# Self-attention without transposes of weights, probabilities and values on TensorE: VectorE turns 32x32 blocks and DMAs inside SBUF place them

## The chip, the cores and the metric

One core of a Trainium2 chip. The metric is the device time of one execution in microseconds.

## The reference

One decoder layer over x of 4 x 512 x 512 in float32. Each of three parts is added to its input and normalised:

```python
k, q, v = W_K x, W_Q x, W_V x                 # 16 heads of 128, float32
scores = causal(q k^T); attn = softmax(scores / sqrt(128))
x = layernorm(x + W_O concat(attn v))
x = layernorm(x + gamma * xattn(x, ctx, ctx)) # 8 heads of 64
xq = activation_quant(rms_norm(x))
x = layernorm(x + (silu(xq sign(W_g)^T) * (xq sign(W_u)^T)) sign(W_d)^T)
```

## The kernel before

The program has four blocks with a barrier between them: constants, `attention` (a loop over 16 heads, four batch items in each, 64 items), `cross_attention` and `ffn`. All data of x stays in SBUF (`acc`). Each float32 operand of a matmul is held as two parts, `hi` (rounded to the matmul's format) and `lo` (the rest), and each product is three matmuls (`SPLIT`: hi hi, hi lo, lo hi).

The order of the work is written by hand, in one instruction stream for each engine; engines meet at semaphores. Every stream has a function `step(h, b)` that holds what it does for item `i = 4h + b`. What TensorE does in a step: the projections K and Q of the next item (12 matmuls of 512 columns each, L355), ten 128x128 transposes of the probabilities of this item (L430), the projection V, at b = 0 and 1 transposes of the signs of the feed-forward weights (L454), z = probabilities times values (L469), the scores of the next item (L368), four transposes of v (L361), and the output projection O (L487). At b = 2 and 3 it also transposes the four weight tiles of the next head (L346), 16 transposes a head. ScalarE copies each PSUM result into its `hi` part (L504) and makes the exponentials (L510); VectorE makes the `lo` parts (L581), turns scores into logits with their row maxima (L590), and adds the output into `acc` (L645). GpSimd does nearly nothing in this block. SP issues all loads; each weight tile is one DMA of 256 KB over 128 partitions.

The signs of the feed-forward weights are made during attention and kept in SBUF, as BF16 (`gT`, `uT`) and as 8-bit integers (`dT`), which ScalarE widens in the first batch of `ffn` (L1252).

The few lines of TensorE's step that set its order of waits:

```python
pe.wait_ge(exp_done, i * NT + NT)          # then the ten transposes
pe.wait_ge(pt_lo, i * len(PT_GROUPS) + (j + 1))   # then z, group by group
pe.wait_ge(z_lo, i + 1)                    # then O
```

## Time and profile before

| | us |
|---|---|
| median of 3 runs | 1622.2 |
| lowest and highest run | 1622.14 and 1622.71 |
| span of the profiled execution | 1621.2 |
| TensorE busy in it | 1574.0 |
| end of the attention stage in it | 1109.5 |

The profiled execution has a span from its first to its last instruction; what lies around the span in a run is 1.0 us by the median. Busy time of TensorE is the time in which some matmul is in its pipeline, so an engine that is always busy need not run at its peak. A wait of an engine that is not the bottleneck costs nothing.

### The profile page before, as it was taken

The page shows a single profiled execution, that of the slowest core. Times are in us where ns is not written, and L with a number is a line of the kernel's source. Part 1 is how long each engine was busy: PE and PEld are TensorE (multiplying, and loading weights), DVE is VectorE, ACT ScalarE, POOL GpSimd, SP SyncE. Part 2 cuts the span into 40 slices and gives each one's busy share as a digit, 9 for nine tenths or more (in the row PEclk, how much of TensorE's full clock was granted, in tenths as well). Part 3 has the DMA queues.
Part 4 walks back from the last instruction along what each step waited for, and adds up shares of the span by engine and source line. Part 5 has one row for each costly group of instructions (what it writes and reads, how often), then busy time and mean ns, then how long its engine had stood idle before and what let it go on. Part 6 is the DMA issues. An engine that isn't in the chain of part 4 may idle for free. (4 is left out here: it accounts for less than half of the span.)

```text
span 1621.2 us, 25726 instructions
## 1 busy us (share of the span) xinstructions
PE 1574.0 (97%) x8332; PEld 1270.9 (78%) x8352; DVE 1014.8 (63%) x2125; ACT 788.7 (49%) x1789; POOL 286.4 (18%) x301
## 2 busy tenths in 40 slices
PE   8999999999999999999999999997999998999997
PEld 7888888888888888888888888885887775565564
DVE  4555555555555555555555555567899996877854
ACT  5444444444444444444444444444888875433332
POOL 0000000000000000000000000004788872433432
PEclk9999999999999999999999999997999999999998
DMA  5000010100101001010010100011111100000000
GB/s 175 29 31 19 26 32 14 44 19 26 32 13 45 19 26 32 13 42 22 26 32 13 32 32 26 2 45 47 52 58 59 40 20 1 1 27 1 26 26 27
DMA packets 40393, 50.85 MB, mean 31 GB/s; under 512 B 3488, under 2 KB 19872, under 8 KB 40352
## 3 DMA queue, kind: packets, MB, share of 16 engines
q1 hardware_dynamic: 40352, 50.35, 9.7%
q8 instruction: 21, 0.34, 0.1%
q14 instruction: 20, 0.16, 0.0%
HBM read 46.14 MB, written 4.19 MB: 31 GB/s over the span
## 5 line engine op out<-in xcount | busy, mean ns | idle before, releaser
L162 POOL TENSOR_TENSOR norm_rstd<-norm_var_eps,minus_half 128x4 f32<-128x4 f32 x12 | 12.2, 1014 | 1116.2 <-DVE norm_var_eps L122 1116.2
L645 DVE SCALAR_TENSOR_TENSOR acc<-attn_bank,prob_recip,acc 128x512 f32<-128x512 f32 x256 | 179.7, 744 | 16.9 <-PE attn_bank L487 16.9
L510 ACT ACTIVATE probs<-probs,neg_max 128x128 f32<-128x128 f32 (+3 forms) x256 | 142.0, 557 | 61.7 <-DVE neg_max L590 61.7
L581 DVE TENSOR_TENSOR zT_lo<-attn_bank,zT_hi 128x512 fp32r<-128x512 f32 x64 | 44.3, 692 | 190.0 <-ACT zT_hi L504 190.0
L504 ACT CAST kT_hi<-attn_bank 128x512 fp32r<-128x512 f32 x64 | 37.5, 587 | 180.3 <-PE attn_bank L355 180.3
L581 DVE TENSOR_TENSOR qT_lo<-attn_bank,qT_hi 128x512 fp32r<-128x512 f32 x64 | 44.2, 691 | 126.0 <-ACT qT_hi L504 125.9
L581 DVE TENSOR_TENSOR kT_lo<-attn_bank,kT_hi 128x512 fp32r<-128x512 f32 x64 | 44.3, 692 | 122.9 <-ACT kT_hi L504 122.9
L1195 PE MATMUL y_bank<-wdT_f32r,prod_hi 128*128 128x512 f32 x256 | 110.8, 433 | 3.0 <-POOL prod_lo L1136 2.5
L1136 POOL TENSOR_TENSOR prod_lo<-prod,prod_hi 128x512 fp32r<-128x512 f32 x64 | 85.6, 1337 | 142.1 <-ACT prod_hi L1244 142.1
L590 DVE CUSTOM_DVE_ANT_0 probs<-attn_bank,mask 128x128 f32<-128x128 f32 (+3 forms) x256 | 109.8, 485 | 0.1
L487 PE MATMUL attn_bank<-woT_hi,zT_hi 128*128 128x512 f32 x256 | 106.2, 415 | 1.6 <-DVE zT_lo L581 1.4
L892 ACT ACTIVATE xprobs<-x_bank,xneg_max 128x512 f32<-128x512 f32 x128 | 88.4, 690 | 38.1 <-DVE xneg_max L956 37.7
L785 POOL TENSOR_SCALAR xprobs<-xprobs,xprob_recip 128x512 f32<-128x512 f32 x128 | 99.5, 793 | 36.5 <-DVE xprob_recip L965 36.5
L504 ACT CAST qT_hi<-attn_bank 128x512 fp32r<-128x512 f32 x64 | 37.7, 589 | 134.7 <-PE attn_bank L355 134.7
L581 DVE TENSOR_TENSOR pT_lo<-attn_bank,pT_hi 128x384 fp32r<-128x384 f32 (+1 forms) x192 | 101.7, 584 | 0.0
L1195 PE MATMUL y_bank<-wdT_f32r,prod_lo 128*128 128x512 f32 x256 | 101.2, 395 | 0.0
L504 ACT COPY vT<-attn_bank 128x512 f32<-128x512 f32 x64 | 37.6, 587 | 129.8 <-PE attn_bank L355 129.8
L487 PE MATMUL attn_bank<-woT_hi,zT_lo 128*128 128x512 f32 x256 | 100.7, 393 | 0.0
L487 PE MATMUL attn_bank<-woT_lo,zT_hi 128*128 128x512 f32 x256 | 99.9, 390 | 0.0
L961 DVE TENSOR_TENSOR xpT_lo<-x_bank,xpT_hi 128x512 fp32r<-128x512 f32 x128 | 87.5, 685 | 7.7 <-ACT xpT_hi L897 5.1
L956 DVE TENSOR_REDUCE xneg_max<-x_bank 128x1 f32<-128x512 f32 x128 | 87.3, 682 | 7.6 <-PE x_bank L826 7.0
L1244 ACT CAST prod_hi<-prod 128x512 fp32r<-128x512 f32 x64 | 39.6, 619 | 99.7 <-DVE prod L1281 98.9
(149 smaller groups left out, 4176.1 us busy)
## 6 DMA issues: line engine op xcount, KB each, us to landing
rows_twice<-in_ctx_dram SPq DMA_DIRECT2D x64, 128.0 KB, 2.6
rows<-in_L_attn_W_K_dram SPq DMA_DIRECT2D x16, 256.0 KB, 2.6
rows<-in_L_attn_W_Q_dram SPq DMA_DIRECT2D x16, 256.0 KB, 2.9
rows<-in_L_attn_W_V_dram SPq DMA_DIRECT2D x16, 256.0 KB, 3.4
rows<-in_L_attn_W_O_dram SPq DMA_DIRECT2D x16, 256.0 KB, 2.7
rows_twice<-in_L_ffn_W_g_dram SPq DMA_DIRECT2D x16, 256.0 KB, 2.7
rows_twice<-in_L_ffn_W_u_dram SPq DMA_DIRECT2D x16, 256.0 KB, 2.8
rows_twice<-in_L_ffn_W_d_dram SPq DMA_DIRECT2D x16, 256.0 KB, 2.7
```

The costliest lines, as they stand in the source:

```text
L487: last_mm = nc.tensor.matmul(O_BANK[t][:], zT[zp][:, t * P:(t + 1) * P], wT["wo"][wp][:], start=(n == 0), stop=(n == 2))
L504: nc.scalar.copy(out, bank[:, 0:cols]).then_inc(done, 1)
L510: nc.scalar.activation(probs[:, cols], probs[:, cols], ACT.Exp, bias=low[:, par, t:t + 1], scale=-1.0, accum_out=total[:, par, t:t + 1]).t ...
L581: nc.vector.tensor_tensor(parts[1][:, at:at + cols], bank[:, 0:cols], parts[0][:, at:at + cols].bitcast(F32), ALU.subtract).then_inc(done, 1)
L590: nc.vector.tensor_tensor_reduce(out=probs[:, s_at[t]:s_at[t] + n], in0=score_bank[bank][:, col:col + n], in1=k.mask[:, S - n:S], scale=-S ...
L645: nc.vector.scalar_tensor_tensor(out=acc[:, b * NT + t, :], in0=O_BANK[t][:], scalar=recip[:, par, t:t + 1], in1=acc[:, b * NT + t, :], op ...
L785: nc.gpsimd.tensor_scalar(probs[q][:, t, :], probs[q][:, t, :], recip[:, q, t:t + 1], 1.0, ALU.mult, ALU.mult).then_inc(probs_ready, 1)
L892: nc.scalar.activation(probs[q][:, t, :], score_bank[t % 2][:], ACT.Exp, bias=negmax[:, q, t:t + 1], accum_out=total[:, q, t:t + 1]).then_ ...
L956: nc.vector.tensor_reduce(negmax[:, q, t:t + 1], score_bank[t % 2][:], AX.X, ALU.max, negate=True).then_inc(max_ready, 1)
L961: nc.vector.tensor_tensor(pT[1][:, jt, :], pt_bank[jt][:], pT[0][:, jt, :].bitcast(F32), ALU.subtract).then_inc(pt_lo, 1)
L1136: nc.gpsimd.tensor_tensor(pT[i][1][:], prod[i][:], pT[i][0][:].bitcast(F32), ALU.subtract).then_inc(p_lo, 1)
L1195: last = nc.tensor.matmul(y_bank[n][:], pT[i][p][:, n * P:(n + 1) * P], wdT[:, t * D:(t + 1) * D], start=(t == 0 and p == 0), stop=(t == N ...
```

## The change

TensorE now transposes only x (at the start) and the quantised activations in `ffn`. Every other transpose is made in two steps. VectorE turns each 32x32 block in place in its 128x128 block (`turn_probs`, `turn_v`, `turn_weight`, `turn_ffn`). Then the 4 x 4 grid of blocks has to be placed: for weights this is done by the load from DRAM, which is now four DMAs over 32 partitions each; for the probabilities and v of an item (ten and four 128x128 blocks, tile `turned`) by 16 DMAs from SBUF to SBUF into `pv..._lo`, each over 32 partitions with 14 runs of 32 floats (128 bytes) in each partition. ScalarE then copies what landed into `pv_hi`, and GpSimd subtracts in place to get `pv_lo`, in two pieces of eight and six blocks. `turned` and both `pv` tiles exist twice. Items are made two ahead (`AHEAD`), one more than before.

The lo parts of weights move to GpSimd too. The signs of the feed-forward weights go to DRAM as they are made and are read back: gate and up at the start of cross-attention, down (as float32) at the start of `ffn`. x and the activations are split into chunks by every fourth column instead of by blocks of 128 columns (`chunk_of`).

```diff
+def chunk_of(x, c):
+    return x.rearrange("p (n c) -> p c n", c=NC)[:, c, :]
...
+        turned = [sb(f"turned{i}", [P, NBLK * P]) for i in range(2)]
+        pv = [[sb(f"pv{i}_{p}", [P, NBLK * P], F32R) for p in ("hi", "lo")] for i in range(2)]
+        zT = [sb(f"zT_{p}", [P, S], F32R) for p in ("hi", "lo")]
+        w_turned = [sb(f"w_turned{i}", [P, D]) for i in range(2)]
+        f_turned = sb("f_turned", [P, D])
...
-        pT = [sb(f"pT_{p}", [P, NPAIR], F32R) for p in ("hi", "lo")]
...
+            def load_projection(eng, name, w, h):
+                w_h = w[bass.ds(h, 1), :, :].rearrange("o (a s) (e j) -> e s (o a) j", s=R, e=E)
+                for e in range(E):
+                    eng.dma_start(raw[name][e * R:(e + 1) * R, :].rearrange("s (a j) -> s a j", a=E),
+                                  w_h[e]).then_inc(w_loaded[name], 16)
...
+            def load_output(eng, h):
+                for e in range(E):
+                    eng.dma_start(raw["wo"][e * R:(e + 1) * R, :].rearrange("s (g r) -> s g r", r=R),
+                                  wo[:, bass.ds(h * DH + e * R, R)].rearrange("(g s) r -> s g r", s=R)).then_inc(w_loaded["wo"], 16)
...
             @block.sync
             def _(sp):
...
+                def exchange(i, par):
...
+                    sp.wait_ge(p_turn, i + 1)
+                    for a in range(E):
+                        for c in range(E):
+                            sp.dma_start(pv[par][1][c * R:(c + 1) * R, :].bitcast(F32).rearrange("r (n a s) -> r n a s", a=E, s=R)[:, :, a, :],
+                                         turned[par][a * R:(a + 1) * R, :].rearrange("r (n c s) -> r n c s", c=E, s=R)[:, :, c, :]).then_inc(landed, 16)
...
+                def keep_signs(h, m):
+                    sp.wait_ge(signed, h * 3 + (m + 2))
+                    if m < 2:
+                        sp.dma_start(signs.gu[m][:, :, bass.ds(h * P, P)], sign_gu[m][:]).then_inc(signs_kept, 16)
+                    else:
+                        sp.dma_start(signs.d[:, bass.ds(h * D, D)], sign_d[:]).then_inc(signs_kept, 16)
...
+                def step(h, b, last):
+                    if not (last and b == B - 1):
+                        exchange(h * B + b + 1, (b + 1) % 2)
+                    if b > 0:
+                        keep_signs(h, b - 1)
+                    if b == 0 and not last:
+                        load_projection(sp, "wk", wk, h + 1)
+                        load_projection(sp, "wq", wq, h + 1)
+                    if b == 1:
+                        wait_apart(sp, k, f_turn, h * 3 + 1)
+                        load_down(sp, h)
+                        if not last:
+                            load_projection(sp, "wv", wv, h + 1)
+                            load_output(sp, h + 1)
+                    if b == B - 1 and not last:
+                        wait_apart(sp, k, f_turn, h * 3 + 3)
+                        load_gate_up(sp, "wg", h + 1)
+                        load_gate_up(sp, "wu", h + 1)
...
             @block.gpsimd
             def _(pool):
...
+                def pieces_lo(i, par):
+                    hi, low = pv[par]
+                    for g, (first, end) in enumerate(PIECES):
+                        cols = slice(first * P, end * P)
+                        pool.wait_ge(pv_hi, i * len(PIECES) + (g + 1))
+                        nc.gpsimd.tensor_tensor(low[:, cols], low[:, cols].bitcast(F32), hi[:, cols].bitcast(F32),
+                                                ALU.subtract).then_inc(pv_lo, 1)
...
             @block.tensor
             def _(pe):
-                def transpose_weights(name, bank):
-                    for c in range(NC):
-                        last = nc.tensor.transpose(bank[:, c * P:(c + 1) * P], raw[name][:, c * P:(c + 1) * P], k.ident[:])
-                    last.then_inc(proj_full, 1)
...
-                def transpose_v(bank):
-                    for j in range(NT):
-                        last = nc.tensor.transpose(bank[:, j * P:(j + 1) * P], vT[:, j * P:(j + 1) * P], k.ident[:])
-                    last.then_inc(proj_full, 1)
+                    last.then_inc(full, 1)
...
                 def step(h, b, last):
-                    more = not (last and b == B - 1)
-                    nb = (b + 1) % B
...
+                    more = not (last and b + AHEAD >= B)
+                    nb = (b + AHEAD) % B
...
-                    pe.wait_ge(exp_done, i * NT + NT)
-                    for g, js in enumerate(PT_GROUPS):
-                        for j in js:
-                            for t in range(j, NT):
-                                at = pt_at[j] - pt_at[js[0]] + (t - j) * P
-                                lt = nc.tensor.transpose(score_bank[g][:, at:at + P],
-                                                         probs[:, s_at[t] + j * P:s_at[t] + (j + 1) * P], k.ident[:])
-                        lt.then_inc(pt_full, 1)
...
-                    if b < 2:
-                        name = ("ffn_gu", "ffn_d")[b]
-                        pe.wait_ge(signed, h * 2 + (b + 1))
...
-                        bank = bank_of(b, name, last)[:].bitcast(BF16)
-                        for m in range((2, 1)[b]):
-                            for c in range(NC):
-                                at = (m * NC + c) * P
-                                lt = nc.tensor.transpose(bank[:, at:at + P], sign_ffn[:, m, c * P:(c + 1) * P], k.ident16[:])
-                        lt.then_inc(proj_full, 1)
...
+                    pe.wait_ge(z_lo, i + 1)
...
-                        if j < len(PT_GROUPS):
-                            pe.wait_ge(pt_lo, i * len(PT_GROUPS) + (j + 1))
+                        if j < len(PIECES):
+                            pe.wait_ge(pv_lo, i * len(PIECES) + (j + 1))
...
-                            last_mm = nc.tensor.matmul(z_bank[:, j * P:S], v[vp][:, j * P:(j + 1) * P],
-                                                       pT[pp][:, pt_at[j]:pt_at[j] + (NT - j) * P],
+                            last_mm = nc.tensor.matmul(z_bank[:, j * P:S], pv[b % 2][vp][:, V_AT[j] * P:(V_AT[j] + 1) * P],
+                                                       pv[b % 2][pp][:, 4 * j * P:(3 * j + NT) * P],
...
                     if more:
-                        pe.wait_ge(proj_lo, lo_count(h, b, "q", last))
-                        scores()
...
+                    pe.wait_ge(z_lo, i + 2)
...
+                    if not (last and b == B - 1):
+                        pe.wait_ge(logits_ready, i * NT + 2 * NT)
...
+                    if more:
+                        pe.wait_ge(v_turn, i + AHEAD)
+                        if new:
+                            pe.wait_ge(w_lo["wv"], h + 2)
+                        project("wv", nb, v_bank, v_full)
...
+                        pe.wait_ge(o_added, i * NT + NT)
+                        scores()
...
             @block.scalar
             def _(act):
...
+                def pieces_hi(i, par):
+                    act.wait_ge(landed, i * (16 * E * E) + 16 * E * E)
+                    for first, end in PIECES:
+                        cols = slice(first * P, end * P)
+                        nc.scalar.copy(pv[par][0][:, cols], pv[par][1][:, cols].bitcast(F32)).then_inc(pv_hi, 1)
...
                 def step(h, b, last):
...
+                    more = not (last and b + AHEAD >= B)
+                    if not (last and b == B - 1):
+                        exps(i + 1, (b + 1) % 2)
                     if more:
-                        group(h, b, "k", last)
...
+                    act.wait_ge(z_full, i + 1)
+                    hi(zT[0][:], z_bank, z_hi)
                     if more:
...
+                        act.wait_ge(q_full, i + AHEAD + 1)
+                        hi(qT[0][:], q_bank, q_hi)
...
+                    if not (last and b == B - 1):
+                        pieces_hi(i + 1, (b + 1) % 2)
...
             @block.vector
             def _(dve):
...
+                def turn_weight(name, n):
...
+                    if not (isinstance(n, int) and n + before == 1):
+                        dve.wait_ge(w_lo[other], n - 1 + before)
+                    dve.wait_ge(w_loaded[name], n * (16 * E))
+                    nc.vector.transpose(*turn_views(w_turned[TMP[name]][:], raw[name][:], name != "wo")).then_inc(w_turn[name], 1)
...
+                def turn_probs(i, par):
+                    for t in range(NT):
+                        dve.wait_ge(exp_done, i * NT + (t + 1))
+                        last = nc.vector.transpose(blocks(turned[par][:], t, 3, t + 1),
+                                                   blocks(probs[:, s_at[t]:s_at[t] + (t + 1) * P], 0, 1, t + 1))
+                    last.then_inc(p_turn, 1)
...
+                def turn_v(i, par, first):
...
+                    dve.wait_ge(v_full, i + 1)
+                    if not first:
+                        dve.wait_ge(landed, i * (16 * E * E) - 16 * E * E)
+                    nc.vector.transpose(blocks(turned[par][:], V_AT[0], V_AT[1] - V_AT[0], 2), blocks(v_bank[:], 0, 1, 2))
+                    nc.vector.transpose(blocks(turned[par][:], V_AT[2], V_AT[3] - V_AT[2], 2), blocks(v_bank[:], 2, 1, 2)).then_inc(v_turn, 1)
...
                 def step(h, b, last):
...
+                    if not (last and b == B - 1):
+                        turn_probs(i + 1, (b + 1) % 2)
+                    if b == 1 and not last:
+                        turn_weight("wk", h + 2)
+                        turn_weight("wq", h + 2)
...
+                        lo(kT, k_bank, k_hi, i + AHEAD + 1, k_lo)
...
+                    lo(zT, z_bank, z_hi, i + 1, z_lo)
+                    if more:
+                        lo(qT, q_bank, q_hi, i + AHEAD + 1, q_lo)
...
-                    for g, js in enumerate(PT_GROUPS):
-                        dve.wait_ge(pt_hi, i * len(PT_GROUPS) + (g + 1))
-                        lo(pT, score_bank[g], pt_at[js[0]], sum(P * (NT - j) for j in js), pt_lo)
...
+                    if b == 1 and not last:
+                        turn_weight("wv", h + 2)
+                    if b == 2 and not last:
+                        turn_weight("wo", h + 2)
+                    if b < 3:
+                        turn_ffn(("wg", "wu", "wd")[b], h, b)
+                    if more:
+                        turn_v(i + AHEAD, par, False)
+                        rows_of_scores(i + AHEAD, par)
...
+                signs.load(sp)
...
+                for t in range(NHT):
+                    sp.dma_start(wdT[:, t * D:(t + 1) * D].bitcast(F32), signs.d[:, t * D:(t + 1) * D]).then_inc(wd_loaded[t], 16)
...
-                            last = nc.tensor.transpose(bank[:, at:at + P], xq[:, t, c * P:(c + 1) * P], k.ident16[:])
+                            last = nc.tensor.transpose(bank[:, at:at + P], chunk_of(xq[:, t, :], c), k.ident16[:])
...
-                        if first:
-                            nc.scalar.copy(wdT[:, t * D:(t + 1) * D], dT[:, t * D:(t + 1) * D]).then_inc(wd_ready, 1)
```

How the order of instructions changed is shown at four places. TensorE before, in the step of the first item: from projection Q of the next item to the transposes of signs (`probs` are the probabilities, `ident` the unit matrix of a transpose).

```order
L355 MATMUL attn_bank<-xT_hi,wqT_lo 128x512 x4
L425 ISA
L430 MATMUL attn_bank<-ident,probs 128x128 x10
L273 REGISTER_ALU
L355 MATMUL attn_bank<-xT_hi,wvT_hi 128x512 x4
L355 MATMUL attn_bank<-xT_lo,wvT_hi 128x512 x4
L355 MATMUL attn_bank<-xT_hi,wvT_lo 128x512 x4
L448 ISA
L273 REGISTER_ALU
L454 MATMUL attn_bank<-ident,sign_ffn 128x128 x8
```

TensorE now, in the same step, between the last matmuls of z and the first of O (`pv` holds the turned probabilities and values).

```order
L466 MATMUL attn_bank<-pv_lo,pv_hi 128x128
L466 MATMUL attn_bank<-pv_hi,pv_lo 128x128
L406 MATMUL attn_bank<-xT_hi,wqT_hi 128x512 x4
L406 MATMUL attn_bank<-xT_lo,wqT_hi 128x512 x4
L406 MATMUL attn_bank<-xT_hi,wqT_lo 128x512 x4
L477 REGISTER_ALU
L479 ISA
L484 MATMUL attn_bank<-woT_hi,zT_hi 128x512
```

No transposes stand there any more; projection Q has moved between z and O, and V and the scores follow behind O.

ScalarE now, in the step b = 1, from the copy of z to the exponentials of the next item (`probs` written with `prob_sum`).

```order
L506 CAST zT_hi<-attn_bank 128x512
L506 CAST qT_hi<-attn_bank 128x512
L512 CAST wqT_hi<-w_turned 128x512
L522 ISA
L525 CAST pv_hi<-pv_lo 128x1024
L525 CAST pv_hi<-pv_lo 128x768
L517 ISA
L518 ACTIVATE probs,prob_sum<-probs,neg_max 128x128
```

Before, the copies of transposed probabilities stood between the projections' copies, each waiting for TensorE. Now one wait (the ISA row at L522) for the 16 transfers stands ahead of the two copies, and the exponentials of the next item follow them.

SP now, in the step b = 1: the 16 transfers, the store of signs, then loads for `wd`, W_V and W_O of the next head.

```order
L298 DMA pv_lo<-turned 32x14x32 x16
L309 ISA
L311 ISA
L311 DMA sign_g_kept<-sign_g 512x1x128
L70 ISA
L288 REGISTER_ALU
L288 DMA rows_twice<-in_L_ffn_W_d_dram 32x16x32
...
L271 DMA rows<-in_L_attn_W_V_dram 32x4x128 x4
L276 ISA
L276 DMA rows<-in_L_attn_W_O_dram 32x16x32
```

Before, SP issued 7 loads in a whole head and one for each tile.

VectorE now, in the step b = 1, from the lo part of z to the turn of v (`w_turned<-rows` is the turn of W_V, and waits for its load).

```order
L695 SCALAR_TENSOR_TENSOR acc<-attn_bank,prob_recip,acc 128x512 x4
L609 STREAM_TRANSPOSE w_turned<-rows 128x512
L612 REGISTER_ALU
L614 STREAM_TRANSPOSE f_turned<-rows_twice 128x512
L640 ISA
L641 STREAM_TRANSPOSE turned<-attn_bank 128x2x128
L642 STREAM_TRANSPOSE turned<-attn_bank 128x2x128
L70 ISA
L621 ISA probs,neg_max<-attn_bank,mask 128x128
```

Before, the scores of the next item were reduced ahead of the adds into `acc`. Now the turns of W_V and of signs stand between the adds and the turn of v, behind which the scores of the item after next are reduced.

## Rows read from the trace of the kernel before

**Rows 1.** The page, part 1: busy us, share of the span, instructions.

```profile
PE 1574.0 (97%) x8332; PEld 1270.9 (78%) x8352; DVE 1014.8 (63%) x2125; ACT 788.7 (49%) x1789; POOL 286.4 (18%) x301
```

**Rows 2.** Windows: us, busy by engine, TensorE clock, DMA share, GB/s.

```profile
0.00:29.68 29.68, 22.91 (x132) 20.04 (x133) 14.15 (x23) 13.60 (x24) 1.97 (x12) 1.00 0.66 230
97.20:164.70 67.50, 67.50 (x371) 57.75 (x370) 36.45 (x84) 30.45 (x73) 0.00 (x0) 1.00 0.09 27
1109.50:1356.50 247.00, 230.23 (x1217) 182.03 (x1216) 225.87 (x408) 193.05 (x447) 186.72 (x213) 0.94 0.15 45
```

**Rows 3.** Waits of the attention stage, 30 to 1109 us: total, times, longest.

```profile
DVE zT_lo L581 <- ACT zT_hi L504: 190.0, 64, 4.0
...
PE attn_bank L469 <- DVE pT_lo L581: 1.1, 1, 1.1
```

**Rows 4.** Timeline of TensorE, one item: start, us, then what ran.

```profile
506.04 1.17 PE L355 MATMUL attn_bank<-xT_hi,wkT_hi 128*128 128x512 f32 x4
...
508.87 1.07 PE L355 MATMUL attn_bank<-xT_hi,wqT_hi 128*128 128x512 f32 x4
...
511.60 1.25 PE L430 MATMUL attn_bank<-ident,probs 128*128 128x128 f32 x10
512.61 1.17 PE L355 MATMUL attn_bank<-xT_hi,wvT_hi 128*128 128x512 f32 x4
...
515.43 0.62 PE L454 MATMUL attn_bank<-ident,sign_ffn 128*128 128x128 bf16 x8
515.86 0.48 PE L469 MATMUL attn_bank<-pT_hi,v_hi 128*128 128x512 f32 x1
...
517.80 0.28 PE L368 MATMUL attn_bank<-kT_hi,qT_hi 128*128 128x128 f32 x1
...
519.77 0.60 PE L361 MATMUL attn_bank<-ident,vT 128*128 128x128 f32 x4
520.12 0.48 PE L487 MATMUL attn_bank<-woT_hi,zT_hi 128*128 128x512 f32 x1
...
522.98 1.07 PE L355 MATMUL attn_bank<-xT_hi,wkT_hi 128*128 128x512 f32 x4
```

**Rows 5.** Groups by line: busy, mean ns of one, idle before.

```profile
L510 ACT ACTIVATE probs<-probs,neg_max 128x128 f32<-128x128 f32 (+3 forms) x256 | 142.0, 557 | 61.7 <-DVE neg_max L590 61.7
...
L538 ACT ACTIVATE sign_ffn<-rows_twice 128x1024 bf16<-128x1024 f32 x8 | 8.5, 1063 | 0.0
...
L581 DVE TENSOR_TENSOR zT_lo<-attn_bank,zT_hi 128x512 fp32r<-128x512 f32 x32 | 22.2, 692 | 97.6 <-ACT zT_hi L504 97.6
...
L1136 POOL TENSOR_TENSOR prod_lo<-prod,prod_hi 128x512 fp32r<-128x512 f32 x64 | 85.6, 1337 | 142.1 <-ACT prod_hi L1244 142.1
```

**Rows 6.** SP's DMA issues: timeline, then min/median/max ns by line, then landing.

```profile
3.98 1.85 SPq L286 DMA_DIRECT2D acc<-in_x_dram  x4
...
1067.31 2.47 SPq L98 DMA_DIRECT2D rows_twice<-in_ctx_dram  x4
...
L94 SPq DMA_DIRECT2D rows<-in_ctx_dram x16: 327/341/505, 1052.7 to 1244.1; - x16
...
L98 SPq DMA_DIRECT2D rows_twice<-in_ctx_dram x64: 465/547/600, 1067.3 to 1317.2; - x64
...
rows_twice<-in_ctx_dram SPq DMA_DIRECT2D x64, 128.0 KB, 2.6
```

**Rows 7.** Windows: the load of one W_O tile (512 packets), and the first loads.

```profile
507.40:509.20 1.80, 1.80 (x10) 1.48 (x9) 0.34 (x1) 0.59 (x2) 0.00 (x0) 1.00 0.58 152
8.00:24.00 16.00, 15.43 (x85) 13.58 (x86) 10.60 (x17) 8.52 (x16) 0.00 (x0) 1.00 1.01 361
```

**Rows 8.** Timeline at the start of cross-attention, SP and GpSimd.

```profile
1113.56 2.79 SPq L98 DMA_DIRECT2D rows_twice<-in_ctx_dram  x4
...
1121.55 0.62 POOL L770 TENSOR_SCALAR cp_hi<-rows_twice 128x512 fp32r<-128x512 f32 x1 [2.83 <-PE x_bank L826]
```

**Rows 9.** Window at the start of cross-attention.

```profile
1110.00:1138.00 28.00, 19.61 (x53) 12.58 (x54) 18.92 (x38) 13.65 (x31) 18.20 (x19) 0.52 0.26 76
```

More of the change, by code:

```diff
@@ L530, in step @@
+                pieces_hi(0, 0)
                 def step(h, b, last):
[L531 removed]
                     i = h * B + b
[L533 to L538 removed]
@@ new lines, in step @@
+                    if b == 2 and not last:
+                        weight_hi("wv", h + 2)
+                    if b > 0:
+                        act.wait_ge(f_turn, h * 3 + b)
+                        act.wait_ge(signs_kept, h * 48 + (16 * b - 15))
+                        if b < 3:
+                            out, x = sign_gu[b - 1][:].rearrange("p c (a s) -> p c a s", a=E), by_chunk(f_turned[:])
+                        else:
+                            out, x = sign_d[:], f_turned[:]
+                        nc.scalar.activation(out, x, ACT.Sign).then_inc(signed, 1)
@@ L1203, in _ @@
                 spread_steps(0)
+                pe.wait_ge(signs.loaded, 32)
                 def batch(b, first, last):
```

546 lines of the change are left out of this document (239 added, 307 removed).

## Prediction

> **What bounds the kernel now.** I read the busy line first, then the stages, then the waits, then one item on TensorE. TensorE is busy for 97% of the span [rows 1]. By stage [rows 2] a head of self-attention takes 67.5 us and TensorE is busy for all of it at granted clock 1.00; cross-attention has 230 of 247 us. The waits of the attention stage say the same from the other side: VectorE idles 190 us in 64 waits for zT_hi alone, while TensorE's one wait for pT_lo is 1.1 us long [rows 3]. So an item of attention costs what its matmuls cost. The profiled span is 1621.2 us, 1.0 us below the median of 1622.2 of the three runs; the sum is made against 1621.2 and 1.0 is added at the end. Faster or slower by 0.2% (3.2 us) is about what such runs can tell from no change.
>
> **TensorE's part.** From the starts in [rows 4], an item is K 2.8, Q 2.7, ten turns of probs 1.0, V 2.8, eight turns of signs 0.4, z 1.9, scores 2.0, four turns of v 0.35, O 2.9. The first matmul behind turns takes some 0.1 longer than its neighbours, so without turns a projection is 2.73, z 1.86, O 2.76, and the item of the changed kernel is 3 x 2.73 + 1.86 + 1.97 + 2.76 = 14.8 us, a head 59.2. Turns, signs and weights thus give back 67.5 - 59.2 = 8.3 us a head, 133 us in 16 heads, if nothing else is late.
>
> **The new path, and the ring it closes.** Between scores and z now stand VectorE, SP's queue, ScalarE and GpSimd. ScalarE works in order: it copies the landed pieces of one item (pieces_hi) and only then makes the exponentials of the next. So one ring runs once per item: landing, two copies, four exponentials, last turn, 16 transfers, landing. Its terms:
> - two copies of 1024 and 768 columns: the sign of 1024 columns took 1.06 us [rows 5], so 1.9 for both.
> - four exponentials of a mean 0.56 [rows 5], which follow one another closely: 2.4 with their gaps.
> - the last turn_probs, 512 columns. No row shows VectorE turning blocks. From below stands the subtraction of 128x512, 0.69 [rows 5], from above twice that, if four-byte blocks run at half rate. I take 0.65 for what delays the ring, since both are one pass over 512 columns; the other end adds 0.6 a ring.
> - a transfer of 57 KB from its issue to landing: 2.6 as the 128 KB loads [rows 6]; that needs its own packets not to be the limit (rival C).
> - 15 issue pitches p on SP. Four 128-partition loads took 1.85 us, so (1.85 - 0.43)/3 = 0.47 apart; four 64-partition loads took 2.47, so (2.47 - 0.59)/3 = 0.63 apart [rows 6]. The median issue is 0.34 against 0.55 us, though the 64-partition load moves half the bytes. The new transfers have 32 partitions, so the 64-partition row is nearest and I take 0.63; 0.47 is the lower end. No row has 32 partitions.
> With handoffs of 0.1 the ring is 7.6 + 15p: 17.0 at 0.63, 14.7 at 0.47. At 0.63 it exceeds TensorE's 14.8; at 0.47 they tie.
>
> The Trainium skill, "VectorE: DVE Perf Modes", section "The three transpose paths", gives 311 ns for a 128x128 two-byte block; by that figure, an estimate, the four blocks of the last turn take up to 1.24, the ring grows by 0.6, and the sum becomes 37 us larger. No run here shows a turn yet.
>
> **What stands behind a new wait.** In step b=1 SP issues 16 transfers, one store of signs, four loads for wd, then four of wv. VectorE, in the same step, waits for that wv load before it turns wv and wu, turns v and reduces the next scores (turn_weight stands ahead of them). At p = 0.63 SP starts 5.0 us into the step, the 25th issue is 24 x 0.63 = 15.1 later and lands 2.6 later, at 22.7; VectorE has finished the adds at 13.9. It waits 9 us, and the turns, the v turn, the reductions, last exponential and last turn of the item behind it (5.7) end at 28.4 where the ring wanted 22.1: 6.3 us late once a head. At 0.47 the same working gives 2.5 + 11.3 + 2.6 = 16.4, then 22.1 against 17.3; slack eats a little, 4.5 remain. Heads: 4 x 17.05 + 6.3 = **74.5**, or 4 x 14.8 + 4.5 = 63.7.
>
> **Ends of the stage.** The loop began at 29.7. Two items are now made ahead, which adds 3 x 2.73 + 1.97 = 10.2; twenty turns of weights and v go, -2.1; the first weights pass SP's and ScalarE's issues, VectorE, ScalarE and GpSimd (its 128x512 subtraction is 1.34 [rows 5]) before the first projection: some 9. Loop start 47. The first z waits 7 more. Two items in the last head have no K, Q, V and scores, -20.3, but their waits for z are uncovered, +8. End: 47 + 7 + 16 x 74.5 - 20.3 + 8 = 1234, against 1109.5: **+124**.
>
> **Behind attention.** The signs of gate and up, 4 MB, are read back ahead of the context rows. At the 361 GB/s of the first loads [rows 7] that keeps the DMA engines for 11.6 us. The GpSimd split that needs rows issued at 1113.6 ran at 1121.6 [rows 8], so 8 of it are covered and 4 to 5 show: +5 (0 to 11). The down signs, 16 loads at the start of the feed-forward, land before use; the 16 casts that ScalarE loses there were beside TensorE: 0. Turning x by every fourth column is a strided weight load that no row shows; 128 such turns, 0 to +6, taken as 0. Stores of signs: hidden, SP time counted above.
>
> **Sum.** 1621.2 + 124 + 5 + 1 = **1751**. With p within 0.60 to 0.66 this case spans 1710 to 1790.
>
> **Rivals.**
> - **B, the issues are quick.** p is 0.47, as for full-width loads. For it: the burst of full-width loads has it, and it is what is left if the width of a transfer does not matter. Against it: every 64-partition row is at 0.47 to 0.60 for the issue alone. Then 45 + 7 + 16 x 63.7 - 20.3 + 9 = 1060, 50 us sooner: 1621.2 - 50 + 5 + 1 = **1577**. The sign turns at p = 0.51, since 0.16 us of p are worth 174. The whole 133 less the ends would be 1503, with p below 0.4 and no wait for wv.
> - **C, small packets are the bound.** A transfer is 448 packets of 128 bytes, 28 for each of the 16 DMA engines. 512 packets of 512 bytes took at most 1.80 x 0.58 x 16 / 512 = 33 ns each [rows 7]. If a 128-byte packet costs as much, a transfer occupies the engines 0.92 us, the ring is 5.0 + 16 x 0.92 + 2.2 = 22 us, a head 91, and the time 1751 + 16 x 16.5 = **2015**. Scaled by bytes alone it would be 0.23 and hidden by p. It decides from 22 ns up. Against it: cost should fall with size at least in part. The Trainium skill, "DMA: Bandwidth & Descriptors", section "Specifications", says that packets under 512 bytes go through a read-modify-write; the same page, in "Why small descriptors are slow (HBM only)", exempts transfers within SBUF. By the first this case is right, by the second it is out; no trace shown here decides.
> - **D, the clock falls.** TensorE is idle a fifth of the time in my case, with waits of 3 to 4 us. Behind the waits at the start of cross-attention the granted clock was 0.52 for 28 us [rows 2, 9], the lower level of 1.2 GHz. One such stretch a head costs 6 to 11 us a head beyond slack: 1850 to 1930. Against it: waits of 1 us at the end of attention changed nothing.
> - **E, it balances** within 0.2%: p within 0.003 of 0.51.
>
> **Chances.** My case 0.45, B 0.31, C 0.13, D 0.08, E 0.03. So faster 0.31, same 0.03, slower 0.66. The range has to reach into B for its 0.31 and up into D; 1560 to 1900 leaves out C (0.13), a quarter of D and about 0.04 of B.
>
> **What would show it.** Right: SP rows of the 16 transfers 0.6 apart, TensorE waiting 2 us before each z for pv_lo, a head near 74 us, VectorE waiting some 9 us for wv once a head, and more DMA packets (7168 an item) at a share under half. B: pitch 0.47, heads near 64. C: DMA share near 1 in the exchanges and landings that grow over the 16. D: a clock below 1.0 in attention. If heads are at 59 the ring is wrong altogether.

## The result, and the profile after

| | before | after |
|---|---|---|
| median, us | 1622.17 (4 runs, 1620.06 to 1622.71) | 1758.14 (4 runs, 1757.77 to 1761.85) |
| ratio to before | | 1.0852, 95% interval 1.0837 to 1.0867 |
| profiled span, us | 1621.2 | 1760.0 |
| start of the loop, us | 29.7 | 56.4 |
| one head in the steady part, us | 67.5 | 74.1 |
| end of self-attention, us | 1109.5 | 1244.8 |
| the rest, us | 511.7 | 515.2 |

The kernel became 8.5% slower: 136 us, against the 129 forecast, and inside the likeliest case's own range of 1710 to 1790. The line numbers below are the changed kernel's, and its copies of landed pieces are line 525.

The page, part 1 (busy us, share of the span, instructions), answers to [rows 1]:

```profile
PE 1526.5 (87%) x7008; PEld 1178.6 (67%) x7008; DVE 1111.8 (63%) x2303; ACT 711.4 (40%) x1549; POOL 637.1 (36%) x493
```

TensorE lost 1324 matmuls and is busy 47 us less, but over a span 139 us longer: no engine is full now. The windows of the start and of one head answer to [rows 2] (us, busy by engine, granted clock, DMA share, GB/s):

```profile
0.00:56.42 56.42, 34.49 (x160) 28.67 (x161) 21.65 (x47) 15.24 (x31) 5.79 (x15) 0.97 0.42 108
493.85:567.97 74.12, 64.34 (x294) 51.66 (x293) 44.07 (x98) 26.10 (x59) 21.85 (x12) 0.98 0.47 81
```

In a head TensorE is idle for 9.8 of 74.1 us; before it was idle for none. The waits (total, times, longest) say for what:

```profile
ACT pv_hi L525 <- DMA pv_lo<-turned: 456.4, 64, 11.0
...
DVE w_turned L609 <- DMA rows<-in_L_attn_W_V_dram: 121.4, 15, 9.0
PE attn_bank L466 <- POOL pv_lo L372: 103.3, 114, 7.7
```

The first two rows shown are the two things that the prediction built on: ScalarE waiting for each of the 64 landings, and VectorE waiting once a head for wv. The long idle time of [rows 3], VectorE's 190 us for z, has shrunk to 92.

The ring, the closed chain of waits that every item goes round once, can be read off three timelines (start us, us, what ran, and in brackets the idle time before it). ScalarE's copies of the landed pieces, one head:

```profile
493.85 1.78 ACT L525 CAST pv_hi<-pv_lo 128x1024 fp32r<-128x1024 f32 x2 [10.38 <-DMA pv_lo<-turned]
510.68 1.78 ACT L525 CAST pv_hi<-pv_lo 128x1024 fp32r<-128x1024 f32 x2 [6.57 <-DMA pv_lo<-turned]
527.48 1.78 ACT L525 CAST pv_hi<-pv_lo 128x1024 fp32r<-128x1024 f32 x2 [6.57 <-DMA pv_lo<-turned]
544.27 1.79 ACT L525 CAST pv_hi<-pv_lo 128x1024 fp32r<-128x1024 f32 x2 [6.01 <-DMA pv_lo<-turned]
567.97 1.79 ACT L525 CAST pv_hi<-pv_lo 128x1024 fp32r<-128x1024 f32 x2 [10.39 <-DMA pv_lo<-turned]
```

Three periods of 16.8 and one of 23.7 make the head of 74.1. Between the second and the third row, ScalarE:

```profile
512.37 0.40 ACT L518 ACTIVATE probs<-probs,neg_max 128x128 f32<-128x128 f32 x1
...
514.57 0.56 ACT L506 CAST kT_hi<-attn_bank 128x512 fp32r<-128x512 f32 x1
```

And SP's queue, whose row of 16 is the exchange of one item:

```profile
515.43 10.62 SPq L298 DMA_DIRECT2D pv_lo<-turned  x16
...
532.23 10.61 SPq L298 DMA_DIRECT2D pv_lo<-turned  x16
543.11 0.63 SPq L311 DMA_DIRECT2D sign_g_kept<-sign_g  x1
544.12 1.95 SPq L288 DMA_DIRECT2D rows_twice<-in_L_ffn_W_d_dram  x4
546.16 1.86 SPq L271 DMA_DIRECT2D rows<-in_L_attn_W_V_dram  x4
...
555.88 10.66 SPq L298 DMA_DIRECT2D pv_lo<-turned  x16
```

So the ring from 510.68 to 527.48 is: copies 1.7, exponentials 2.2, last turn 0.9 (514.57 to 515.43), from the first issue to the start of the last 10.0 (the row's 10.62 less one issue of 0.62, the median), landing 2.05. Sum 16.8. The exception is the item after 544.27. VectorE's own row for it, and the turns of probabilities behind it:

```profile
549.83 1.11 DVE L609 STREAM_TRANSPOSE w_turned<-rows 128x512 f32<-128x512 f32 x1 [8.51 <-DMA rows<-in_L_attn_W_V_dram]
...
554.14 1.72 DVE L632 STREAM_TRANSPOSE turned<-probs 128x128 f32<-128x128 f32 x4
```

The wv load ends with the 25th issue, at 548.0, and has landed at 549.8; everything behind it on VectorE, the reductions that ScalarE's exponentials need among it, is late, and the exchange starts at 555.88.

### The profile page after: what moved, and what is told of

Its sections match the earlier page's. It is cut to its first block and busy times, and to the rows that moved or that the text cites. A ratio compares the mean times of both kernels' runs of the same rounds, so it can differ in the third digit from the quotient of the medians.

```text
span 1760.0 us, 24483 instructions
## 1 busy us (share of the span) xinstructions
PE 1526.5 (87%) x7008; PEld 1178.6 (67%) x7008; DVE 1111.8 (63%) x2303; ACT 711.4 (40%) x1549; POOL 637.1 (36%) x493
## 5 line engine op out<-in xcount | busy, mean ns | idle before, releaser
L372 POOL TENSOR_TENSOR pv_lo<-pv_lo,pv_hi 128x1024 fp32r<-128x1024 f32 (+1 forms) x128 | 267.7, 2113 | 685.2 <-ACT pv_hi L525 685.2
L525 ACT CAST pv_hi<-pv_lo 128x1024 fp32r<-128x1024 f32 (+1 forms) x128 | 114.2, 940 | 456.4 <-DMA pv_lo<-turned 456.4
L466 PE MATMUL attn_bank<-pv_hi 128*128 128x512 f32 (+3 forms) x256 | 96.0, 375 | 103.5 <-POOL pv_lo L372 103.3
L632 DVE STREAM_TRANSPOSE turned<-probs 128x128 f32<-128x128 f32 (+3 forms) x256 | 124.6, 504 | 87.4 <-ACT probs L518 81.4
L484 PE MATMUL attn_bank<-woT_hi,zT_hi 128*128 128x512 f32 x256 | 115.2, 450 | 66.5 <-DVE zT_lo L595 66.5
L466 PEld LDWEIGHTS attn_bank<-pv_hi 128*128 128x128 f32 x256 | 51.7, 202 | 154.6 <-POOL pv_lo L372 142.9
L609 DVE STREAM_TRANSPOSE w_turned<-rows 128x512 f32<-128x512 f32 x64 | 61.8, 983 | 130.8 <-DMA rows<-in_L_attn_W_V_dram 121.4
L484 PE MATMUL attn_bank<-woT_lo,zT_hi 128*128 128x512 f32 x256 | 112.9, 441 | 0.0
L484 PEld LDWEIGHTS attn_bank<-woT_hi,zT_hi 128*128 128x128 f32 x256 | 55.4, 216 | 85.1 <-issue 66.7
L484 PE MATMUL attn_bank<-woT_hi,zT_lo 128*128 128x512 f32 x256 | 112.0, 438 | 0.0
```

The costliest lines, as they stand in the source:

```text
L372: nc.gpsimd.tensor_tensor(low[:, cols], low[:, cols].bitcast(F32), hi[:, cols].bitcast(F32), ALU.subtract).then_inc(pv_lo, 1)
L466: last_mm = nc.tensor.matmul(z_bank[:, j * P:S], pv[b % 2][vp][:, V_AT[j] * P:(V_AT[j] + 1) * P], pv[b % 2][pp][:, 4 * j * P:(3 * j + NT) ...
L484: last_mm = nc.tensor.matmul(s_bank[t][:], zT[zp][:, t * P:(t + 1) * P], wT["wo"][wp][:], start=(n == 0), stop=(n == 2))
L525: nc.scalar.copy(pv[par][0][:, cols], pv[par][1][:, cols].bitcast(F32)).then_inc(pv_hi, 1)
L632: last = nc.vector.transpose(blocks(turned[par][:], t, 3, t + 1), blocks(probs[:, s_at[t]:s_at[t] + (t + 1) * P], 0, 1, t + 1))
```

## The experiments

The kernel before was timed beside each. Its medians beside the timed runs were 1620.35 to 1621.61 (1618.42 in one run beside E6).

### E1: the wv load one step earlier

```diff
                     if b == 0 and not last:
...
                         load_projection(sp, "wq", wq, h + 1)
+                        load_projection(sp, "wv", wv, h + 1)
                     if b == 1:
...
-                            load_projection(sp, "wv", wv, h + 1)
                             load_output(sp, h + 1)
```

> Only the four loads of wv are moved, from behind the loads of wd in step b=1 to behind those of wk and wq in step b=0. Theory 1 (a ring of landing, copies, exponentials, turn and 16 issues, 16.8 us, and once a head the wait of VectorE for wv stretches it to 23.7): the wait (9 us, 15 times) is gone, all four periods are 16.8, the head 67.2 to 68, and the time 1758 - 16 x 6.5 = 1654, within 1640 to 1665. Theory 2 (SP's queue is full over the head, 64 transfers and 28 other issues, and the wait for wv only shows it): the four issues now push the exchange of step b=1 back by what they save later, and the time stays within 1750 to 1765.

Measured: 1654.47 us, ratio to before 1.0207 (1.0190 to 1.0224). In the steady part all periods are now 16.8; two of ScalarE's copies:

```profile
502.91 1.79 ACT L525 CAST pv_hi<-pv_lo 128x1024 fp32r<-128x1024 f32 x2 [6.07 <-DMA pv_lo<-turned]
519.75 1.78 ACT L525 CAST pv_hi<-pv_lo 128x1024 fp32r<-128x1024 f32 x2 [6.62 <-DMA pv_lo<-turned]
```

The single place of one load was worth 103.7 us. Only 15 of the 16 heads load weights for a next one (the wait for wv is there 15 times), so that is 6.9 for each of them, what the long period had over the others. The same number of issues stands on SP's queue, so theory 2 falls: it is not the load of the queue but who waits behind which issue.

### E6: what an issue costs

Bursts alone, no layer. The kinds differ in the pair of views given to each transfer.

> The layer is left out; only bursts of 16 transfers of 56 KB (one kind 28 KB) follow one another, each kind twice, each burst awaited before the next: (1) 32 partitions x 14 pieces of 128 bytes between quadrants, as the changed kernel has them, (2) the same with 7 pieces, (3) 32 partitions x one run of 1792 bytes, (4) 128 partitions x one run of 448 bytes, (5) 64 partitions x 14 pieces, twice the bytes, (6) 32 x 14 pieces read from DRAM in one run a partition; then (1) on ScalarE's queue, and at the end half of it on each queue at once. Theory A (the number of partitions sets the issue, as the prediction reasoned): (1), (2), (3), (6) have the same pitch, 0.6 to 0.7, and (4) 0.47. Theory B (the number of packets that an issue makes sets it): (2) and (3) are at 0.35 to 0.5, (1) and (6) at 0.6 to 0.7, (5) above 1.0. Packets: 12 ns each by the busy share of 0.52 in an exchange of 10.5 us, so (5) is bound by packets at 16 x 896 / 16 x 12 ns = 10.9 us, no longer than its issues. Last burst: two queues together take 5.5 to 6 us if packets bound it, 5.3 if issues do, 10.6 if the queues share one path.

Each burst's second run, in the timeline of SP (start us, us, what ran; 16 issues each, the last row 8), in order: 14 pieces, 7 pieces, one run of 1792 bytes, 128 partitions x 448 bytes, 64 partitions x 14 pieces, from DRAM, half of the 14 pieces on SP:

```profile
18.65 10.59 SPq L1468 DMA_DIRECT2D landing<-turned  x16
42.29 10.35 SPq L1468 DMA_DIRECT2D landing<-turned  x16
65.62 10.00 SPq L1468 DMA_DIRECT2D landing<-turned  x16
88.46 10.12 SPq L1468 DMA_DIRECT2D landing<-turned  x16
112.93 11.30 SPq L1468 DMA_DIRECT2D landing<-turned  x16
135.92 8.13 SPq L1468 DMA_DIRECT2D landing<-in_x_dram  x16
170.68 5.62 SPq L1468 DMA_DIRECT2D landing<-turned  x8
```

ScalarE's queue, with all of the 14 pieces alone, and with its half beside SP's last row:

```profile
158.43 10.76 ACTq L1468 DMA_DIRECT2D landing<-turned  x16
170.62 5.39 ACTq L1468 DMA_DIRECT2D landing<-turned  x8
```

Neither theory holds. Half the packets, a fourteenth of them, or four times the partitions change the pitch by 6% at most (0.67, 0.65, 0.63, 0.64), and twice the partitions and bytes cost 0.71. Of the kinds tried only the one that reads from DRAM is quicker: 0.52. Two queues issue at once at 0.72 and 0.68. DRAM as the source is not enough for a quick issue, though: the 64-partition context loads of [rows 6] read from it too and are 0.63 apart. Windows over the same bursts (the share is the last number but one), for the 14 pieces, the 7 pieces, the one run, 128 partitions, 64 partitions, and both queues:

```profile
18.65:31.00 12.35, 0.00 (x0) 0.00 (x0) 1.00 0.45 74
42.29:54.00 11.71, 0.00 (x0) 0.00 (x0) 1.00 0.24 39
65.62:77.00 11.38, 0.00 (x0) 0.00 (x0) 1.00 0.33 81
88.46:100.00 11.54, 0.00 (x0) 0.00 (x0) 1.00 0.29 80
112.93:125.90 12.97, 0.00 (x0) 0.00 (x0) 1.00 0.84 142
170.68:177.70 7.02, 0.00 (x0) 0.00 (x0) 1.00 0.81 131
```

A DMA engine gets 448 packets in the first: 12.35 x 0.45 / 448 = 12.4 ns for one of 128 bytes; 11.71 x 0.24 / 224 = 12.5 and 12.97 x 0.84 / 896 = 12.2 for the 7 pieces and the 64 partitions. That is the price of rival C, which needed 22. The same bytes in runs of 1792 bytes keep the engines busy for 11.38 x 0.33 = 3.8 us, in runs of 448 bytes for 11.54 x 0.29 = 3.3, in pieces of 128 bytes for 12.35 x 0.45 = 5.6: small packets cost 1.5 to 1.7 times as much here, but the 10.0 us of issues hide it. One exchange occupies the engines for 5.6 us, so two queues at 8 issues each are almost at that bound as well: share 0.81.

### E2 and E3: half of the transfers on ScalarE's queue

`exchange_part(eng, i, par, parts)` is the old `exchange` over some source quadrants; SP calls it for 0 and 1.

```diff
                         exps(i + 1, (b + 1) % 2)
+                        exchange_part(act, i + 1, (b + 1) % 2, range(2, E))
                     if more:
                         act.wait_ge(k_full, i + AHEAD + 1)
```

> Half of the 16 transfers of an item (source quadrants 2 and 3) are issued by ScalarE, right behind its four exponentials, the other half by SP as before. Theory 1 (the pitch of the issues on one queue bounds the ring): 8 x 0.665 = 5.3 us leave the ring, 11.5 is below TensorE's 14.8, and a head takes 60 to 63 us: time 1530 to 1580. Theory 2 (the packets bound it: 16 DMA engines are busy for 0.52 of 10.5 us in an exchange, 5.5 us for 448 packets each): two queues finish no sooner than the engines can, but 5.5 us is still half of 10.6, so the ring is near 12 and the time is the same within 10 us; had the busy share hidden waits inside the engines (a packet bound below 1.0), the landing would stay 12 us behind the first issue and the time at 1740 to 1760. Theory 3: ScalarE's own issues of 5.3 us delay its copies of k and q, and the head stays above 68: 1660 or more.

> The edits of the wv load and of the two queues together. Theory 1: TensorE sets the pace with 14.8 us an item, a head 59.5 to 61, and the time is 1515 to 1545, below the kernel before (1622). Where the granted clock stays near 1.0, the lower end. Rival (clock): TensorE still meets the lower clock behind its waits and the head stays above 64: 1590 or more.

Measured: E2 1872.75 us (ratio 1.156, 1.1538 to 1.1582), E3 (with E1's edit) 1875.74 (1.1562, 1.1541 to 1.1582). Both are slower than the changed kernel, and 0.2% apart: E1's edit gives nothing here. ScalarE in E2:

```profile
495.42 0.40 ACT L520 ACTIVATE probs<-probs,neg_max 128x128 f32<-128x128 f32 x1 [7.02 <-DVE neg_max L625]
...
498.65 5.69 ACTq L295 DMA_DIRECT2D pv_lo<-turned  x8
504.45 0.59 ACT L508 CAST kT_hi<-attn_bank 128x512 fp32r<-128x512 f32 x1 [6.59 <-issue]
...
505.99 0.57 ACT L508 CAST zT_hi<-attn_bank 128x512 fp32r<-128x512 f32 x1
...
515.90 0.40 ACT L520 ACTIVATE probs<-probs,neg_max 128x128 f32<-128x128 f32 x1 [6.66 <-DVE neg_max L625]
```

ScalarE no longer waits for a landing but for the next scores. The issues hold up the copy of z, which TensorE had ready at 500.6; its output projection waits for it, at 507.42:

```profile
507.42 0.78 PE L486 MATMUL attn_bank<-woT_hi,zT_hi 128*128 128x512 f32 x1 [3.87 <-DVE zT_lo L599]
508.00 0.63 PE L486 MATMUL attn_bank<-woT_lo,zT_hi 128*128 128x512 f32 x1
508.43 0.63 PE L486 MATMUL attn_bank<-woT_hi,zT_lo 128*128 128x512 f32 x1
```

A new ring: exponentials, turn, 8 issues, four copies, O, V, scores, reduction, exponentials: 20.5 us from 495.42 to 515.90. Theory 3 was right in kind and too small: it counted the copy of z with those of k and q, and not what TensorE still has to run behind it. The output projection also starts with matmuls 0.43 us apart, where they are 0.23 apart at clock 1.00: behind the wait of 3.9 the granted clock was 0.52 (507.42 to 510.94), the lower level.

### E5: the exponentials ahead of the copies

```diff
                         exps(i + 1, (b + 1) % 2)
+                    pieces_hi(h * 2 + (b // 2 + 1), b % 2)
...
-                    if not (last and b == B - 1):
-                        pieces_hi(i + 1, (b + 1) % 2)
```

> ScalarE makes the exponentials of item i+1 ahead of the copies of the landed pieces of item i (its wait for the landing moves behind them; one landing count for each parity). Theory 1 as forecast (the ring closes through ScalarE's order alone): with it broken an item costs TensorE's 14.8, or SP's 13 to 14 of issues, the head 60 to 66 with the wv wait, time 1535 to 1630. Theory 2 (behind it lies a second ring, from the scores through reduction 0.7, exponentials 2.2, turn 0.8, issues 10.6, landing 2.2, copy 0.95 and split 2.1 to z, two steps later and 2.7 into the step): about 17.9 + 0.5 - 2.7 = 15.7 an item, a head 63 plus 4 to 7 for wv, 67 to 70, time 1650 to 1695. Theory 3 (SP's queue bounds): no change, 1750 to 1765.

Measured: 1897.59 us, 1.1716 (1.1688 to 1.1744), a miss of all three theories. ScalarE:

```profile
499.18 0.40 ACT L518 ACTIVATE probs<-probs,neg_max 128x128 f32<-128x128 f32 x1 [5.98 <-DVE neg_max L619]
...
501.53 1.77 ACT L525 CAST pv_hi<-pv_lo 128x1024 fp32r<-128x1024 f32 x2
...
522.91 0.40 ACT L518 ACTIVATE probs<-probs,neg_max 128x128 f32<-128x128 f32 x1 [7.69 <-DVE neg_max L619]
```

And TensorE's first matmul of z:

```profile
505.08 0.50 PE L466 MATMUL attn_bank<-pv_hi 128*128 128x512 f32 x1 [2.41 <-POOL pv_lo L372]
```

The last issue for these pieces had ended at 493.7, 7.9 us before their copy began at 501.53. But z could now start only behind the exponentials and the copies of its pieces, 5.9 us after 499.18, and the scores of the next item stand behind z, Q, O and V in TensorE's order: 14 to 18 us more. Four items in a row took 19.5, 23.7, 19.9 and 20.0. In the one of 23.7, shown here, VectorE also waits 1.7 us for wv, and TensorE ran at granted clock 0.50 from 506.86 to 512.60, so that its projection Q took 4.8 us instead of 2.8. The order of the changed kernel, copies first, was the better one. Breaking one ring closed another.

### E7 and E9: the same issues where ScalarE idles

In the changed kernel ScalarE idles 2.2 us between the copies of z and q and 6.6 behind the copy of q. Both kernels have E1's edit, and SP issues the transfers that ScalarE does not. E7:

```diff
+                        exchange_part(act, i + 1, (b + 1) % 2, range(3, E))
                         pieces_hi(i + 1, (b + 1) % 2)
```

> The wv load in step b=0 as in e1_wv_early; the four transfers of the last source quadrant are issued by ScalarE at the end of its step, behind its copy of q and ahead of its wait for the landing, where it idled 6.6 us in e1_wv_early; SP issues the other 12. Theory 1 (issues on one queue bound the ring, and e2_two_queues lost because 5.7 us of issues stood ahead of the copies of k, z and q): SP's last issue comes 7.3 us behind its first instead of 10.0, ScalarE's last 7.6 behind it, the landing 2.2 later: the ring falls from 16.8 to 14.7, TensorE's 14.8 takes over, a head is 59.5 to 62 and the time 1654 - 16 x 6.3 = 1553, within 1535 to 1580, below the kernel before (1622). Theory 2 (two queues at once slow each other, as landings of 3.5 us in e2_two_queues against 2.2 may say): the landing comes 1.3 later, ring 16.0, time 1654 - 16 x 3 = 1605, 1590 to 1630. Theory 3 (z's wait for the split of the pieces is on TensorE's own path whatever the ring): above 1640.

Measured: **1534.17 us**, ratio 0.9467 (0.9452 to 0.9483). E9 counts `parts` in single transfers:

```diff
                     hi(zT[0][:], z_bank, z_hi)
+                    if not (last and b == B - 1):
+                        exchange_part(act, i + 1, (b + 1) % 2, range(10, 13))
...
+                        exchange_part(act, i + 1, (b + 1) % 2, range(13, E * E))
                         pieces_hi(i + 1, (b + 1) % 2)
```

> As e7_act_4, but SP issues 10 transfers, ScalarE three between its copies of z and q (2.2 us idle there) and three behind the copy of q. Theory 1: the last issue is 6.9 us behind SP's first, ring 14.0, below TensorE's 14.8, so TensorE alone sets the pace: head 59.5 to 61, time 1530 to 1560, and at or up to 15 us below e7_act_4. Rival: the three issues of 0.7 ahead of the copy of q delay q, and with it the scores of the item two ahead: slower than e7_act_4 by up to 64 x 0.6 = 40 us.

Measured: **1524.43 us**, ratio 0.9416 (0.9392 to 0.9440): 5.8% below the kernel before, and the fastest here. The window of one head of E9:

```profile
493.18:552.53 59.35, 59.16 (x289) 50.18 (x289) 42.03 (x96) 27.26 (x59) 22.11 (x12) 1.00 0.61 101
```

TensorE is busy for 59.16 of 59.35 us, at clock 1.00: the 59.2 that the prediction worked out for an item without turns. E7 missed its forecast of 1553 on the good side, because it counted 60.9 us a head, and a head took 59.8, TensorE busy for all but 0.05 of it. Two queues at once do slow the landing (a median of 2.7 and 2.8 us in E9, 2.2 in the changed kernel), but the slack covers that: what lost in E2 was not the second queue as such. The Trainium skill, "Perfetto Trace Analysis", section "DMA Optimizations", advises to balance transfers over the engines that can issue them when making descriptors is the limit. E9 agrees with it, with 1524 us; E2, with 1873, shows what it leaves out.

### E10: E9 with the wv load back in its place

> As e9_act_3_3, but the wv load is back where the changed kernel has it (step b=1, behind the loads of wd). Theory 1: in that step SP starts 4.9 us in, its 19th issue (10 transfers, a store, 4 for wd, 4 for wv) is 11.5 later and lands 2.0 after that, at 18.4; VectorE is free at 13.9, waits 4.5, and the exchange behind it starts 4 us later than TensorE alone would have it: 1524 + 16 x 4 = 1588, within 1565 to 1600. Rival: without the ring this wait lies in slack: under 1535.

Measured: 1585.41 us, 0.9778 (0.9761 to 0.9794), 61 us above E9, 4.1 for each of the 15 heads that load a next wv. The copies start at 494.23, 509.33, 523.75, 538.14 and 557.30: one period of 19.2 among three of 14.4 to 15.1. The wait for wv costs even where no ring bounds, only less: 4.1 us a head here, 6.9 in E1's comparison.

### E11: eight of the transfers late on ScalarE

E3 with `exchange_part(act, ...)` moved to the place that it has in E7.

> As e3_both (wv early, 8 of the 16 transfers issued by ScalarE), but ScalarE issues them at the end of its step, behind the copy of q, as in e7_act_4. Theory 1 (e3_both lost by the place of the issues, not by their number or by two queues at once): the copies of k, z and q are free again; ScalarE's last issue comes 5.5 + 7 x 0.7 = 10.4 us behind SP's first, where SP alone had 10.0, so the ring is about 17.2 and the time 1654 + 64 x 0.4 = 1680, within 1650 to 1710. Theory 2 (eight transfers on each of two queues slow each other): near e3_both, above 1800.

Measured: 1754.19 us, 1.0821 (1.0784 to 1.0859). The place alone gave back 121 us of E3's 1875.74, but the forecast of 1680 was 74 too low. Two neighbouring items (windows: us, busy by engine, granted clock, DMA share, GB/s):

```profile
504.78:525.33 20.55, 17.70 (x72) 14.43 (x71) 10.26 (x23) 6.13 (x14) 5.38 (x3) 0.83 0.47 83
486.60:504.78 18.18, 17.07 (x82) 13.84 (x81) 10.60 (x28) 6.16 (x15) 4.20 (x2) 1.00 0.53 94
```

One ran at clock 1.00 in 18.2 us, the other at 0.83 in 20.5. ScalarE's eight issues stand behind the copy of q and end the exchange, so TensorE's z and Q are inside the ring. (With four, in E7, SP's last issue was the later one: 480.56 against 480.10 in one item.) In the slower item z follows a wait of 2.0 us, and the copy of q comes 4.6 us behind that of z instead of 2.8. This is rival D at work, in a ring that passes through TensorE.

The clock is the smaller part of the miss, though. Of 62 periods in the stage, 36 ran at clock 1.00 and still took 18.1 us on average, 0.9 above the forecast's 17.2; the other 26 took 19.0. In the item of 18.2 the issues are as forecast, but the copy begins at 504.78, 3.2 us behind the start of ScalarE's last issue, where the forecast had 2.2 for the landing. So theory 2 was true in part. SP issues weight loads in the same stretch, and whether they or the second queue delay the landing is not shown.

## Why the prediction was right, and where it was not

**The ring: right, and nearly to the tenth.** Forecast 17.05, measured 16.8. The pitch was taken as 0.63 and is 0.667; the landing was taken as 2.6 and is 2.05; the copies were 1.7 against 1.9, the exponentials 2.2 against 2.4. The last turn, for which no row existed, was taken as 0.65 and delays the ring by 0.86; the turn of 512 columns itself lasts 0.71. These errors cancel to 0.25, and that is luck: the pitch alone added 0.55 a ring, and lies outside the 0.60 to 0.66 for which the prediction had 1710 to 1790; the landing took 0.55 off again.

**The estimate from the Trainium skill, "VectorE: DVE Perf Modes", section "The three transpose paths",** (311 ns for a 128x128 two-byte block, so 1.24 for four) was too high. One 128x128 block of four-byte values took 0.31, the page's figure for two-byte ones, but four blocks in one instruction took 0.71. A price for one instruction must not be multiplied by its blocks.

**The pitch: the right number for a wrong reason.** I chose the 64-partition row because the new transfers are narrow. But the weight loads of the changed kernel, which have 32 partitions too, issue in half the time, and four of them in 1.74 us are 0.47 apart (min/median/max ns by line):

```profile
L271 SPq DMA_DIRECT2D rows<-in_L_attn_W_K_dram x60: 316/317/464, 80.0 to 1121.6; - x60
...
L298 SPq DMA_DIRECT2D pv_lo<-turned x1024: 586/624/1461, 51.4 to 1228.5; - x171
```

E6 shows a pitch of 0.63 to 0.67 at 32 and at 128 partitions when the source is SBUF. By the argument on width alone, a reader of the same rows could as well have come to 0.47 and rival B: the choice that decided between slower and faster was lucky. What makes these transfers slower to issue is not known; E6 has one kind only that reads from DRAM, and the 0.63 of the context loads fits neither width nor source.

**What stands behind the wait for wv: right.** SP's wv load was to land 22.7 us into the step, and did at 549.83 - 527.48 = 22.35. The next exchange was to start at 28.4, and did at 555.88 - 527.48 = 28.4. Forecast 6.3 us late once a head; the period is 6.9 longer, and E1 gives 6.9 back in each head that has the wait.

**TensorE's part: right.** 59.2 a head, shown by E9. So the change's idea was sound: of the 133 us in the heads, E9 brings 96 in the whole kernel, with a loop that starts 27 us later than before. In the changed kernel they were lost to 16 issues in a row on one queue and to one load behind them.

**The start: a term too small.** The loop was to start at 47 and did at 56.4. TensorE was idle ahead of its first projections:

```profile
21.33 2.04 PE L406 MATMUL attn_bank<-xT_hi,wkT_hi 128*128 128x512 f32 x4 [10.79 <-DVE xT_lo L655]
28.82 1.99 PE L406 MATMUL attn_bank<-xT_hi,wqT_hi 128*128 128x512 f32 x4 [2.07 <-POOL wqT_lo L365]
```

The first projection starts at 21.3 where it had started at 13.9, 7.5 later, where the term said 9. But its four matmuls take 2.04 instead of 1.20 behind the idle 10.8 us, and those of Q 1.99 instead of 1.18 behind another wait; K and Q together take 3.5 us more than before. For Q the granted clock is 0.52 (28.82 to 32.31). For K the matmuls are as far apart, but the profile gives 1.00 there, so the clock is not shown as the cause. Three waits of 1.0 to 2.1 us that were not there before add 4.7. None of this was in the sum. The first z then waited 7.73 (forecast 7). No run was spent on the start.

**The end: a term of the wrong kind.** With loop start, heads and first wait as measured, the sum's last line would end attention at 1237; it ended at 1244.8. The sum took 20.3 us off for the matmuls that the last two items do not have, and put 8 back for waits. But the ring set the pace, not TensorE. ScalarE's last two copies:

```profile
1213.22 1.78 ACT L525 CAST pv_hi<-pv_lo 128x1024 fp32r<-128x1024 f32 x2 [6.57 <-DMA pv_lo<-turned]
1230.56 1.78 ACT L525 CAST pv_hi<-pv_lo 128x1024 fp32r<-128x1024 f32 x2 [9.23 <-DMA pv_lo<-turned]
```

They are 17.3 us apart, no less than elsewhere, though TensorE has no K, Q, V and scores there, and the stage ends 14.2 behind the last one. So the two items save some 2 us, not 12.3. The output projections run at 0.43 us a matmul behind waits of 4.7 and 1.4, granted clock 0.52 and 0.57. Against that the sum charged the wait for wv to 16 heads, and 15 have it: 6.9 too much. The rest is some 4 us of single periods that were longer than 16.8 and 23.7.

**Behind attention:** forecast +5 and 0, measured 515.2 - 511.7 = +3.5. The error of the whole, 1758 against 1751, is start +9.4, first z +0.7, heads -6.4, end +7.4, the rest -1.5; the median also lies 1.9 below the profiled span, where the sum had put it 1.0 above. That the total is within 7 us owes something to terms of opposite sign.

**The rivals.** B fell with the pitch. C fell with 12.4 ns a packet. The two sections of "DMA: Bandwidth & Descriptors" of the Trainium skill that the prediction weighed are thereby decided for this kernel: by "Why small descriptors are slow (HBM only)" transfers within SBUF do not suffer the penalty of small packets. The measured 12.4 ns agree in that rival C is out, but not fully, since the same bytes in larger runs took 3.3 to 3.8 us of the engines against 5.6. D came half true. In the changed kernel the granted clock is 0.98 in the head shown and 0.94 over the loop, and an output projection behind a wait of 4.07 starts at the lower level (0.52 from 557.96 to 561.48, the matmuls 0.43 apart, then 0.23):

```profile
557.96 0.77 PE L484 MATMUL attn_bank<-woT_hi,zT_hi 128*128 128x512 f32 x1 [4.07 <-DVE zT_lo L595]
```

But its ring does not pass through TensorE, so this fell into slack: the period from 344.98 to 361.78 had granted clock 0.80, that from 510.68 to 527.48 had 1.00, and both took 16.8 us. In E11 the ring did pass through TensorE, and of two neighbouring items the one at the lower clock took 2.4 us longer.

## What to carry to other kernels

Write down the whole ring of an item, across engines and queues, and for each engine what stands behind a waiting or issuing instruction: moving one load within SP's order gave 104 us here, moving six issues to ScalarE's idle stretches gave 130 more, and eight issues at a wrong place in ScalarE's order cost 115. When the bound engine's work shrinks, the next bound is often not another engine but one queue's issue pitch times the number of transfers; count the transfers first, and give some to a queue whose engine is idle at that moment. Reordering to break one ring closes another, so trace the new order through all engines before the edit.

## What was not expected of the hardware

- The pitch of issues on one queue hardly depends on a transfer's size: 0.67 us for 448 packets, 0.65 for 224, 0.63 for 32, 0.71 for 896, all from SBUF; 0.52 for 448 from DRAM. In the layer the weight loads from DRAM (4 in 1.74 to 1.98 us) are some 0.5 apart, the context loads 0.63.
- Two queues issue side by side at 0.72 and 0.68, and 128-byte packets within SBUF cost a DMA engine 12.4 ns, 1.5 to 1.7 times the time of the same bytes in larger runs.
- A turn of 32x32 blocks of four-byte values takes 0.31 us for 128 columns, 0.43 for 256, 0.57 for 384, 0.71 for 512, about 0.13 for each 128 columns more. With the strided views of the projections' weights the same 512 columns take 1.07, against 0.70 for the unstrided wo.
